# A two-round graph network on one core: the rows that TensorE gathers are made four halves ahead instead of eight

## The chip, the cores and the metric

The kernel runs on one core of one Trainium2 chip. The metric is the device time of one execution, in microseconds (us). The kernel before takes 5044.6 us, the median of three runs (5039.53, 5044.60 and 5044.64).

## What is computed

There are 12500 nodes of 16 numbers and 400000 edges, each with a source node, a target node and 13 edge features. The targets are sorted. The reference, cut to what matters:

```
w = relu(edge_attr @ w1 + b1) @ w2 + b2        # per edge a 16 x 16 matrix W, once
for _ in range(2):                             # two rounds
    m   = einsum('ei,eio->eo', hx[edge_src], W)
    agg = segment_sum(m, edge_dst) / max(degree, 1)
    hx  = gru_cell(agg, hx)                    # two 16 x 48 matrices, sigmoid, tanh
out = layernorm(x + hx)
```

The change is in `hx[edge_src]`, the gather of the source rows.

## The kernel before

**Tiles.** The edges are cut into tiles of 128. 64 tiles are a super (NSUP = 49 supers), and a super is worked off in 8 halves of 8 tiles, k = 0 to 7. Each of the two rounds runs over the 49 supers. The loops are unrolled for the first pair of supers and for the last super (`for_supers`, L420), so `is_first` means super 0 of a round and `is_last` means super 48. In time, the supers are counted through here: 0 to 48 are those of round 0 and 49 to 97 those of round 1.

**A half, engine by engine.** The gathered rows of a half lie in xg. VectorE multiplies them with a one-hot of the target's place in a window into `fan` (`spread`, L1184). TensorE multiplies `fan` with the hidden layer of the edges (`products`, L805). In round 0 TensorE also makes the hidden layer of the next super (`hidden`, L780), which is stored to h_d by SP (L513) and loaded again in round 1 (L529). At places of a super set by k, TensorE also runs `own_sums` (k = 0 and 6), `aggregate` (k = 0), `turn` (k = 2) and `scatter` (k = 4 and 5).

**Two ways to gather.** Of the 8 tiles of a half, POOL gathers 5 (or 4) by one indirect DMA each (L598), and TensorE makes the other 3 (or 4; `BY_PE`, L33: 24 tiles a super in round 0, 26 in round 1). For these, ScalarE makes a one-hot of the sources from the broadcast keys (`src_hots`, L655: four Abs and one Relu). TensorE multiplies it with the node table in SBUF, seven matmuls a tile (`gather_rows`, L783). VectorE picks the row out of 28 candidates (`pick_rows`, L1222, one instruction a tile) with a mask made once a super (`rows_hot`, L1210), and sums (`keep_rows`, L1230, one a half). TensorE's tiles are made one super ahead: during half k of super s, those of half k of super s + 1. So super 0 of a round has none made by TensorE: POOL gathers all its 64 tiles (`pool_places`, L106), and the last super has no gather work on TensorE. There it runs the 12 node-side gate products instead, 2 a half from k = 2 (`side_gates`, L856), and ScalarE copies them out (`keep_sides`, L673).

**What sets the order.** Each engine has its own list of instructions and waits on semaphores. POOL may run LEAD = 4 halves ahead of `products` (L595). VectorE's order in a half is: spread, one-hot of the next half, keep_hot, (add_windows at k = 5 and 6), pick and keep of the gather of the half before, `rows_hot` at k = 0, and `places` at k = 2. In supers 0 and 1 of round 0 it also runs `relative` (L1125 to L1130) in each half.

**SP's queue.** SP issues, for super `sup`: the indices (L473), the features (L485), the keys of super sup + 1 (L506), then in round 0 the store of the hidden layer, in round 1 its load. Ahead of the keys it waits that the buffer is free:

```
wait_pos(sp, s_src_hot, pe_total(rnd) if is_first(i, par) else pe_count(rnd, sup, 0))   # L503
```

In super 1 of round 0 there follow, behind the keys, `loads_of_later()` (L446: 15 small `lane` copies, `meta`, 8 `slot_of` broadcasts, weights), the first store to h_d, and two DMAs that zero the accumulator acc_all (L519). VectorE waits for these at the end of super 0: `places_of_tiles()`, then `dve.wait_ge(s_acc, 32)` (L1302). After this comes the drain that tells all engines that the super is done.

Of the kernel before, what the change touches and what calls it, by code (L numbers as in the profile page):

```python
# [5 lines left out]
P = 128  # L6
# [27 lines left out]
LEAD = 4  # L34
DUO = 2
# [11 lines left out]
KB = 4  # L47
# [14 lines left out]
def gnn_program(nc, x, x_t, src_tiles, src_pe_rows, src_pe_cols, dst_rows, dst_tiles, ef_t, w1_diag, w2_io, w2_oi,  # L62
# [30 lines left out]
    assert 6 * GW <= PICKED and GN <= SLOTS * C * AR and 4 * GN <= TG * P * 4 // 2 * 2  # L93
    assert NSUP % 2 == 1 and NSUP <= P and GROUPS * C == P and 2 * GN == NT and C == 16
# [24 lines left out]
    def keys_use(rnd, i, par):  # L119
        buf, use = ring(rnd, i, par)  # L120
        return use - sum(ring(r, 0, 0)[0] == buf for r in range(rnd + 1))
# [20 lines left out]
    with ExitStack() as ctx:  # L142
# [229 lines left out]
        SIDE_FROM, SIDE_EACH = 2, 2  # L372
# [62 lines left out]
        def is_last(i):  # L435
            return isinstance(i, int) and i == PAIRS

# [7 lines left out]
        def _(sp):  # L445
# [21 lines left out]
            for rnd in range(ROUNDS):  # L467
                def emit(i, par, rnd=rnd):
# [150 lines left out]
        def _(act):  # L619
# [35 lines left out]
            def src_hots(rnd, i, par, s, k):  # L655


                buf, use = ring(rnd, i, par)
                first, some = sum(GT[:k + 1]) - BY_PE[rnd][k], BY_PE[rnd][k]
                if k == 0:  # L660
                    act.wait_ge(s_keys[buf], 16 * keys_use(rnd, i, par))
                if k > 1:
                    act.wait_ge(s_g, pe_count(rnd, s, sum(BY_PE[rnd][:k - 1])))
                else:
                    wait_pos(act, s_g, pe_count(rnd, s, 0) - (1 - k) * (0 if isinstance(s, int) and s == 1 else BY_PE[rnd][HPS - 1]))
# [3 lines left out]
                act.wait_ge(s_src_far, KB * (HPS * (rnd * (NSUP - 1) + s - 1) + k + 1))  # L669
# [43 lines left out]
            for rnd in range(ROUNDS):  # L713

                def emit(i, par, rnd=rnd):
                    sup = rnd * NSUP + 2 * i + par
                    buf, _ = ring(rnd, i, par)
                    for k in range(HPS):
                        if k == 0 and not is_last(i):
                            src_hots(rnd, i + par, 1 - par, 2 * i + par + 1, 0)  # L720
                        if k == 0 and not is_first(i, par):
                            keep_agg(sup - 1)
                        if k > 0 and k + 1 < HPS and not is_last(i):
                            src_hots(rnd, i + par, 1 - par, 2 * i + par + 1, k + 1)
# [9 lines left out]
                        if not is_last(i) and k == 0:  # L734
# [799 lines left out]
```

## Time and profile before

| what | us |
|---|---|
| median of the runs (3) | 5044.6 |
| span of the profiled execution, first to last instruction | 5034.4 |
| median less span (start and end of the program) | 10.2 |
| round 0 to the first fan of its last super | 0 to 2493.8 |
| last super of round 0, its tail and the node update | 2493.8 to 2584.2 |
| first super of round 1 (super 49) | 2584.2 to 2662.2 |
| rest of round 1 to the first fan of the last super | 2662.2 to 4942.8 |
| last super of round 1 and the end | 4942.8 to 5034.4 |

The time of the profiled execution itself is not given apart from its span; the sum is made against the span, and what lies around the span is taken as unchanged. In the tables of busy time a window runs from the first fan of a super to the next stage's first fan. In the timeline a line gives the start, the time taken, the engine and line of code, what is written and read, how many instructions are merged, and in brackets how long the engine sat idle before it and what ended that.

### The profile page before, as it was taken

The numbers are of one execution on the slowest core, as the hardware profiler recorded it, in microseconds if no ns is written. First come the engines' busy times: TensorE is split into PE (matmuls) and PEld (weight loads), VectorE is DVE, ScalarE is ACT, GpSimd is POOL, SyncE is SP. The second block draws the span as 40 slices with busy tenths as digits, with TensorE's granted clock in tenths as the row PEclk, the third lists the DMA queues.
The fourth block names the chain that finished last, engine by engine and source line by source line (L and its number), as shares of the span: only waits on it lengthen the run. The fifth ranks groups of instructions, "written<-read, shape, count | busy, mean of one in ns | idle before, by whom it ended". The sixth has DMA issues, their size and how long they took to land.

```text
span 5034.4 us, 125092 instructions
## 1 busy us (share of the span) xinstructions
PE 4872.1 (97%) x41816; PEld 4032.3 (80%) x41817; DVE 4440.1 (88%) x6732; ACT 3310.7 (66%) x5283; POOL 3666.9 (73%) x3879
## 2 busy tenths in 40 slices
PE   6999999999999999999969999999999999999997
PEld 4788888878888878888748888888888888888885
DVE  8888888888888888888848999999999999999996
ACT  4667676766666666666636767667677676766763
POOL 7677777777777777777757777777777777777773
PEclk9999999999999999999979999999999999999998
DMA  6122222212122212121111111111111111111110
GB/s 164 46 58 53 56 55 55 56 51 61 50 62 50 61 46 65 46 65 46 51 50 55 39 55 39 55 55 39 55 39 55 55 40 55 39 55 46 48 48 17
DMA packets 193534, 269.20 MB, mean 53 GB/s; under 512 B 93601, under 2 KB 161796, under 8 KB 180065
## 3 DMA queue, kind: packets, MB, share of 16 engines
q1 hardware_dynamic: 62353, 223.38, 13.4%
q0 software_dynamic: 123584, 31.88, 6.1%
q8 instruction: 373, 6.11, 0.5%
q10 hardware_dynamic: 7026, 6.21, 0.5%
q14 instruction: 198, 1.62, 0.1%
HBM read 201.25 MB, written 54.94 MB: 51 GB/s over the span
## 4 chain that ended last, share of the span: by engine, by line
PE 91%; issue 3%; DVE 3%; POOL 2%; DMA 1%; DVEq 0%; POOLq 0%; ACT 0%; ACTq 0%; SPq 0%
PE ps_all L793 58%; PE ps_all L805 10%; PE ps_all L795 9%; PE ps_all L780 5%; PE ps_all L828 4%; PE ps_all L849 2%; POOL xg L598 2%; PE ps_all L819 1%; PE ps_all L835 1%; DVE shared L1222 1%; DVE fan L1184 1%; DVE xg L1230 0%; DMA acc_all<-in_dst_rows 0%; DMA stat_all<-low_d 0%; PE ps_all L854 0%
## 5 line engine op out<-in xcount | busy, mean ns | idle before, releaser
L793 PE MATMUL ps_all<-parts,src_hot 128*128 128x448 f32 x14400 | 3417.8, 373 | 8.2 <-DVEq L1108 7.0
L793 PEld LDWEIGHTS ps_all<-parts,src_hot 128*128 128x128 f32 x14400 | 2665.4, 188 | 324.5 <-issue 103.3
L598 POOL DMA_INDIRECT xg<-in_x,idx x1979 | 1874.6, 947 | 641.5 <-issue 554.6
L598 POOL DMA_INDIRECT xg<-h_rows,idx x1883 | 1777.3, 944 | 627.2 <-issue 532.1
L667 ACT ACTIVATE src_hot<-keys,neg_key 128x384 fp32r<-128x384 int16 (+1 forms) x3072 | 1680.3, 620 | 794.9 <-PE ps_all L795 785.8
L1222 DVE TENSOR_TENSOR shared<-ps_all,at_hot 128x448 f32<-128x448 f32 x2400 | 1390.2, 616 | 287.3 <-PE ps_all L795 264.9
L1230 DVE TENSOR_REDUCE xg<-shared 128x48 f32<-128x1344 f32 (+1 forms) x768 | 1237.5, 1611 | 81.8 <-DVE shared L1222 3.3
L1184 DVE TENSOR_TENSOR fan<-xg,ps_all 128x1280 f32<-128x1280 f32 x784 | 1159.5, 1479 | 119.7 <-DMA xg<-h_rows,idx 49.1
L671 ACT ACTIVATE src_hot<-src_hot 128x1536 fp32r<-128x1536 f32 (+1 forms) x768 | 1184.9, 1543 | 74.4 <-ACT src_hot L667 8.2
L795 PE MATMUL ps_all<-parts,src_hot 128*128 128x448 f32 x2400 | 878.8, 366 | 0.0
L805 PE MATMUL ps_all<-fan,h_sb 128*32 128x160 f32 x12544 | 592.6, 307 | 82.9 <-DVE fan L1184 80.5
L805 PEld LDWEIGHTS ps_all<-fan,h_sb 128*32 128x32 f32 x12544 | 328.7, 109 | 338.6 <-issue 274.0
L795 PEld LDWEIGHTS ps_all<-parts,src_hot 128*128 128x128 f32 x2400 | 451.5, 188 | 37.6
L639 ACT COPY shared<-ps_all 128x320 f32<-128x320 f32 x784 | 326.9, 417 | 234.7 <-PE ps_all L805 234.6
L645 ACT COPY agg_sb<-ps_all 128x160 f32<-128x160 f32 x98 | 28.7, 293 | 484.3 <-PE ps_all L828 484.3
L780 PE MATMUL ps_all<-w_sb,ef 105*128 105x264 f32 x784 | 285.7, 447 | 29.0 <-DMA ef<-in_ef_t 20.8
L828 PE MATMUL ps_all<-shared,w2s 128*64 128x160 f32 x3136 | 240.3, 307 | 1.9 <-issue 1.9
L780 PEld LDWEIGHTS ps_all<-w_sb,ef 105*128 105x128 f32 x784 | 119.0, 191 | 131.2 <-issue 117.8
L828 PEld LDWEIGHTS ps_all<-shared,w2s 128*64 128x64 f32 x3136 | 209.9, 139 | 7.4 <-issue 2.2
L1172 DVE TENSOR_TENSOR ps_all<-ps_all,rel 128x80 f32<-128x80 f32 x784 | 189.8, 242 | 0.2 <-DVE ps_all L1161 0.2
L1191 DVE COPY hot_sb<-ps_all 128x80 f32<-128x80 f32 x784 | 180.2, 230 | 0.0
L633 ACT ACTIVATE h_sb<-ps_all 128x264 f32<-128x264 f32 x392 | 154.2, 393 | 30.0 <-PE ps_all L780 24.3
(135 smaller groups left out, 1284.8 us busy)
## 6 DMA issues: line engine op xcount, KB each, us to landing
keys<-key_d SPq DMA_DIRECT2D x96, 832.0 KB
h_d<-h_sb SPq DMA_DIRECT2D x49, 1056.0 KB
h_sb<-h_d SPq DMA_DIRECT2D x49, 1056.0 KB
xg<-in_x,idx POOLq DMA_INDIRECT x1979, 2.3
xg<-h_rows,idx POOLq DMA_INDIRECT x1883, 2.3
ef<-in_ef_t SPq DMA_DIRECT2D x49, 420.0 KB
acc_all<-agg_t SPq DMA_DIRECT2D x1, 3161.0 KB
idx<-in_src_tiles SPq DMA_DIRECT2D x98, 32.0 KB, 1.8
```

Of the source, the lines that this page charges most:

```text
L598: pool.indirect_dma_start(out=xg[:, buf, at, 0:C], out_offset=None, in_=rows_of, in_offset=bass.IndirectOffsetOnAxis(ap=idx[:, buf, at:at ...
L639: act.copy(pev[:, :, 2 * k:2 * k + 2, :].rearrange("p i u n -> p u i n"), ps_p[k % 2][:, 0:2 * C * WIN].rearrange("p (u i n) -> p u i n", ...
L667: act.activation(src_hot[k % 2][:, kb, 0:some * P], keys[:, buf, first * P:(first + some) * P], ACT.Abs, bias=neg_key[:, kb:kb + 1]).then_ ...
L671: act.activation(hot_of, hot_of.bitcast(F32), ACT.Relu, bias=1.0, scale=-1.0).then_inc(s_src_hot, some)
L780: pe.matmul(ps_h[:, 0:HT * HA], ef[:, buf, k, :], w1_sb[:], start=True, stop=True).then_inc(s_h, 1)
L793: pe.matmul(ps_g[j], src_hot[k % 2][:, kb, j * P:(j + 1) * P], parts[:, m * WHOLE + kb, :], start=(kb == 0 and m == 0), stop=False)
L795: last = pe.matmul(ps_g[j], src_hot[k % 2][:, WHOLE, j * P:(j + 1) * P], tail_part, start=False, stop=True)
L805: last = pe.matmul(ps_p[k % 2][b * HID:(b + 1) * HID, u * C * WIN:(u + 1) * C * WIN], h_sb[:, buf, k * HT + u * BPS + b, 0:HID], fan[:, k ...
L828: last = pe.matmul(ps_agg[lo:lo + BPS * C, 0:TPB * WIN], w2s[:, i, :], pev[:, i].rearrange("p t n -> p (t n)"), start=(i < 2), stop=(i >= ...
L1184: dve.tensor_tensor(fan[:, k % 2], xg[:, buf, k * HT:(k + 1) * HT, 0:C].unsqueeze(3).to_broadcast([P, HT, C, WIN]), hot[:, k % 2].unsqueez ...
L1222: dve.tensor_tensor(picked[:, j], ps_g[j].rearrange("p (a c) -> p c a", a=AR), at_hot[:, u].unsqueeze(1).to_broadcast([P, C, AR]), ALU.mul ...
L1230: dve.tensor_reduce(xg[:, buf, at:at + many, 0:C], picked[:, 0:many], AX_X, ALU.add).then_inc(s_xg_pe, many)
```

## The change

The gather on TensorE runs EARLY = 4 halves ahead: during half k, the rows of half k + 4 are made, of the same super for k < 4 and of the next one for k >= 4. Halves 4 to 7 of super 0 of each round then have 3 or 4 tiles made by TensorE, and so do not need POOL for them. The gather of the last super's halves 4 to 7 is made in its halves 0 to 3. The side gates move from 2 a half from k = 2 to 4 a half from k = 5. `rows_hot` for super 0 runs at k = 0 of super 0, that for super s + 1 at k = 4 of super s. SP loads the keys of super 0 too, and its wait ahead of the keys counts the tiles anew: `pe_count(rnd, sup, 0)` is 12 larger than before in round 0 (12 tiles of super 0 are counted now, of its 24), so for super 1 it asks for 12 where it asked for 0.

```diff
+EARLY = 4
+SIDE_FROM, SIDE_EACH = 5, 4
     def pool_places(rnd, s, k):
-        made = 0 if isinstance(s, int) and s == 0 else BY_PE[rnd][k]
+        made = 0 if isinstance(s, int) and s == 0 and k < EARLY else BY_PE[rnd][k]
...
+    def skipped(rnd):
+        return sum(BY_PE[rnd][:EARLY])
 
     def pe_total(rnd):
-        return (NSUP - 1) * sum(sum(BY_PE[r]) for r in range(rnd))
+        return sum(NSUP * sum(BY_PE[r]) - skipped(r) for r in range(rnd))
 
     def pe_count(rnd, s, n):
-        return pe_total(rnd) + (s - 1) * sum(BY_PE[rnd]) + n
+        return pe_total(rnd) + s * sum(BY_PE[rnd]) + n - skipped(rnd)
...
-        SIDE_FROM, SIDE_EACH = 2, 2
...
+        def rows_for(i, par, k):
+
+            if k + EARLY < HPS:
+                return i, par, k + EARLY
+            return None if is_last(i) else (i + par, 1 - par, k + EARLY - HPS)
+
+        def rows_before(i, par, k):
+
+            if k > 0:
+                return rows_for(i, par, k - 1)
+            return None if is_first(i, par) else (i, par, EARLY - 1)
+
+        def rows_next(i, par, k):
+
+            if k + 1 < HPS:
+                return rows_for(i, par, k + 1)
+            return None if is_last(i) else (i + par, 1 - par, EARLY)
...
                     if not is_last(i):
                         wait_pos(sp, s_src_hot, pe_total(rnd) if is_first(i, par) else pe_count(rnd, sup, 0))
-                        if is_first(i, par) and rnd > 0:
-                            sp.wait_ge(s_rz_sum, NS * rnd)
+                        if is_first(i, par):
+                            if rnd > 0:
+                                sp.wait_ge(s_rz_sum, NS * rnd)
+                            sp.dma_start(keys[:, buf, :], key_d[0:1, :].to_broadcast([P, TG * P])).then_inc(
+                                s_keys[buf], 16)
...
-                        if k == 0 and not is_last(i):
-                            src_hots(rnd, i + par, 1 - par, 2 * i + par + 1, 0)
+                        if k == 0 and is_first(i, par):
+                            src_hots(rnd, *rows_for(i, par, 0))
...
-                        if k > 0 and k + 1 < HPS and not is_last(i):
-                            src_hots(rnd, i + par, 1 - par, 2 * i + par + 1, k + 1)
+                        if k > 0 and rows_next(i, par, k):
+                            src_hots(rnd, *rows_next(i, par, k))
...
-                        if not is_last(i) and k == 0:
-                            src_hots(rnd, i + par, 1 - par, 2 * i + par + 1, 1)
+                        if k == 0:
+                            src_hots(rnd, *rows_next(i, par, k))
...
-                        if not is_last(i):
+                        if rows_for(i, par, k):
                             if is_first(i, par) and k == 0:
                                 pe.wait_ge(s_parts, rnd + 1)
-                            gather_rows(rnd, s + 1, k)
+                            gather_rows(rnd, *rows_for(i, par, k))
...
+                        made = rows_before(i, par, k)
+                        if made:
+                            pick_rows(rnd, *made, (0, 1))
...
+                        if made:
+                            pick_rows(rnd, *made, (2, 3))
+                            keep_rows(rnd, *made)
...
-                        if not is_last(i) and k == 0:
+                        if is_first(i, par) and k == 0:
+                            rows_hot(rnd, 0)
+                        if not is_last(i) and k == EARLY:
                             rows_hot(rnd, s + 1)
```

Left out of the diff are the waits of `src_hots`, `gather_rows`, `pick_rows` and `rows_hot`, which take the new counts.

## Rows read from the trace of the kernel before

**Rows 1.** The page: busy time of each engine, and the chain that ended last.

```profile
PE 4872.1 (97%) x41816; PEld 4032.3 (80%) x41817; DVE 4440.1 (88%) x6732; ACT 3310.7 (66%) x5283; POOL 3666.9 (73%) x3879
PE 91%; issue 3%; DVE 3%; POOL 2%; DMA 1%; DVEq 0%; POOLq 0%; ACT 0%; ACTq 0%; SPq 0%
```

**Rows 2.** Busy time by stage: PE, PEld, DVE, ACT, POOL, granted clock, DMA share, GB/s.

```profile
2443.40:2493.80 50.40, 50.40 (x429) 40.98 (x429) 43.89 (x66) 33.25 (x57) 37.78 (x41) 1.00 0.20 48
2493.80:2524.00 30.20, 23.92 (x283) 14.75 (x281) 21.03 (x37) 9.15 (x21) 18.83 (x20) 0.94 0.14 40
2584.20:2662.20 78.00, 50.90 (x327) 41.50 (x328) 45.84 (x78) 33.49 (x48) 58.89 (x63) 0.81 0.11 23
4894.50:4942.80 48.30, 48.30 (x428) 41.40 (x426) 45.38 (x68) 31.51 (x46) 35.86 (x38) 1.00 0.13 31
4942.80:4971.00 28.20, 22.63 (x284) 14.29 (x282) 21.54 (x38) 9.06 (x21) 16.99 (x18) 1.00 0.19 36
```

**Rows 3.** Waits of the whole run (page, costliest groups): what fan waits for.

```profile
L1184 DVE TENSOR_TENSOR fan<-xg,ps_all 128x1280 f32<-128x1280 f32 x784 | 1159.5, 1479 | 119.7 <-DMA xg<-h_rows,idx 49.1 <-DVE xg L1230 44.5 <-issue 17.7
```

**Rows 4.** Timeline at the start of round 1: POOL's issues, and fans of super 49.

```profile
2574.43 0.94 POOL L598 DMA_INDIRECT xg<-h_rows,idx  x1 [0.30 <-issue]
...
2614.46 1.49 DVE L1184 TENSOR_TENSOR fan<-xg,ps_all 128x1280 f32<-128x1280 f32 x1 [4.02 <-DMA xg<-h_rows,idx]
...
2654.49 1.49 DVE L1184 TENSOR_TENSOR fan<-xg,ps_all 128x1280 f32<-128x1280 f32 x1 [5.01 <-DMA xg<-h_rows,idx]
```

**Rows 5.** SP's issues in super 0 of round 0.

```profile
39.38 0.62 SPq L506 DMA_DIRECT2D keys<-key_d  x1
...
59.21 18.20 SPq L519 DMA_DIRECT2D acc_all<-agg_t  x2
```

**Rows 6.** Busy time in two short windows of super 0; last but one is the DMA share.

```profile
95.00:100.00 5.00, 5.00 (x55) 4.22 (x53) 4.76 (x8) 2.10 (x4) 3.78 (x5) 1.00 0.43 92
100.00:105.00 5.00, 4.54 (x34) 3.62 (x34) 4.83 (x11) 3.42 (x7) 3.78 (x5) 1.00 0.07 10
```

**Rows 7.** Timeline of super 0: ScalarE's fourth one-hot, and VectorE's end of the super.

```profile
70.51 1.49 ACT L671 ACTIVATE src_hot<-src_hot 128x1536 fp32r<-128x1536 f32 x1
...
106.50 0.42 DVE L1152 TENSOR_SCALAR slot_of<-slot_of,lane 128x392 f32<-128x392 f32 x1
```

**Rows 8.** Timeline of a steady super of round 1: halves 5 to 7, then rows_hot at k = 0.

```profile
3673.04 1.69 DVE L1222 TENSOR_TENSOR shared<-ps_all,at_hot 128x448 f32<-128x448 f32 x3
...
3674.41 1.47 PE L793 MATMUL ps_all<-parts,src_hot 128*128 128x448 f32 x6
...
3678.50 1.68 DVE L1222 TENSOR_TENSOR shared<-ps_all,at_hot 128x448 f32<-128x448 f32 x3
...
3679.52 1.48 PE L793 MATMUL ps_all<-parts,src_hot 128*128 128x448 f32 x6
...
3688.35 0.91 DVE L1210 TENSOR_TENSOR at_hot<-ps_all,at_pe 128x728 f32<-128x728 f32 x1
...
3689.18 1.48 DVE L1184 TENSOR_TENSOR fan<-xg,ps_all 128x1280 f32<-128x1280 f32 x1
```

**Rows 9.** Waits of L1222, ten steady supers of round 0, then twelve of round 1.

```profile
DVE shared L1222 <- PE ps_all L795: 47.4, 79, 1.8
...
DVE shared L1222 <- PE ps_all L795: 12.8, 36, 0.5
```

**Rows 10.** Timeline of the last super of round 0: two gathers, first and last products, gates.

```profile
2493.64 1.38 PE L793 MATMUL ps_all<-parts,src_hot 128*128 128x448 f32 x6
...
2495.07 1.38 PE L793 MATMUL ps_all<-parts,src_hot 128*128 128x448 f32 x6
...
2496.58 0.75 PE L805 MATMUL ps_all<-fan,h_sb 128*32 128x160 f32 x16
...
2521.86 0.75 PE L805 MATMUL ps_all<-fan,h_sb 128*32 128x160 f32 x16 [2.48 <-DVE fan L1184]
...
2522.54 1.58 PE L854 MATMUL ps_all<-mh,gate_w 128*128 128x392 f32 x4
```

More of the change, by code:

```diff
@@ L93, in gnn_program @@
     assert 6 * GW <= PICKED and GN <= SLOTS * C * AR and 4 * GN <= TG * P * 4 // 2 * 2
+    assert EARLY % 2 == 0 and 0 < EARLY < HPS and SIDE_FROM > HPS - EARLY
     assert NSUP % 2 == 1 and NSUP <= P and GROUPS * C == P and 2 * GN == NT and C == 16
@@ L117, in landed, with starts_round @@
         return i * (16 * usual) + 16 * (earlier + usual + first + last)
-    def keys_use(rnd, i, par):
-        buf, use = ring(rnd, i, par)
-        return use - sum(ring(r, 0, 0)[0] == buf for r in range(rnd + 1))
+    def skipped(rnd):
+        return sum(BY_PE[rnd][:EARLY])
     def pe_total(rnd):
-        return (NSUP - 1) * sum(sum(BY_PE[r]) for r in range(rnd))
+        return sum(NSUP * sum(BY_PE[r]) - skipped(r) for r in range(rnd))
     def pe_count(rnd, s, n):
-        return pe_total(rnd) + (s - 1) * sum(BY_PE[rnd]) + n
+        return pe_total(rnd) + s * sum(BY_PE[rnd]) + n - skipped(rnd)
+    def starts_round(s, k):
+        return isinstance(s, int) and s == 0 and k == EARLY
     def slot_free(rnd, k, j):
@@ L653, in keep_turned, with src_hots @@
                              s_agg_t, 1)
[L655 removed]
+            def src_hots(rnd, i, par, k):
                 buf, use = ring(rnd, i, par)
+                s = 2 * i + par
                 first, some = sum(GT[:k + 1]) - BY_PE[rnd][k], BY_PE[rnd][k]
[L660 to L662 removed]
+                if k == 0 or starts_round(s, k):
+                    act.wait_ge(s_keys[buf], 16 * use)
+                if isinstance(s, int) and s == 0 and k < EARLY + 2:
+                    wait_pos(act, s_g, pe_total(rnd))
+                elif k > 1:
                     act.wait_ge(s_g, pe_count(rnd, s, sum(BY_PE[rnd][:k - 1])))
                 else:
[L665 removed]
+                    act.wait_ge(s_g, pe_count(rnd, s, 0) - (1 - k) * BY_PE[rnd][HPS - 1])
                 for kb in range(KB):
@@ L781, in hidden, with gather_rows @@
                           start=True, stop=True).then_inc(s_h, 1)
-            def gather_rows(rnd, s, k):
+            def gather_rows(rnd, i, par, k):
+                s = 2 * i + par
                 for j, (n, _, _) in enumerate(pe_tiles(rnd, k)):
                     pe.wait_ge(s_src_hot, pe_count(rnd, s, n) + 1)
-                    if isinstance(s, int) and s == 1 and slot_free(rnd, k, j) < 0:
+                    if isinstance(s, int) and s == 0 and slot_free(rnd, k, j) < skipped(rnd):
                         wait_pos(pe, s_picked, pe_total(rnd))
@@ L1181, in spread @@
                 dve.wait_ge(s_xg[buf][k], landed(rnd, i, par, k))
-                if not is_first(i, par):
+                if not (is_first(i, par) and k < EARLY):
                     dve.wait_ge(s_xg_pe, pe_count(rnd, 2 * i + par, sum(BY_PE[rnd][:k + 1])))
@@ L1207, in rows_hot @@
             def rows_hot(rnd, s):
-                wait_pos(dve, s_picked, pe_count(rnd, s, 0))
+                wait_pos(dve, s_picked, pe_total(rnd) if isinstance(s, int) and s == 0 else pe_count(rnd, s, 0))
                 dve.tensor_tensor(at_hot[:], iota_ps[:, 0:AR].unsqueeze(1).to_broadcast([P, TG, AR]),
@@ L1212, in rows_hot, with pick_rows @@
                                   ALU.is_equal).then_inc(s_at_hot, 1)
-            def pick_rows(rnd, s, k, js):
+            def pick_rows(rnd, i, par, k, js):
+                s = 2 * i + par
                 for j, (n, u, _) in enumerate(pe_tiles(rnd, k)):
                     if j in js:
-                        if n == 0:
-                            dve.wait_ge(s_at_hot, rnd * (NSUP - 1) + s)
+                        if n == 0 or j == 0 and starts_round(s, k):
+                            dve.wait_ge(s_at_hot, rnd * NSUP + s + 1)
                         dve.wait_ge(s_g, pe_count(rnd, s, n) + 1)
```

17 lines of the change are left out of this document (3 added, 14 removed).

## The prediction

> **What bounds the kernel now.** I read the page first: TensorE is busy 97% of the span and 91% of the chain that ended last [rows 1]. A mean over stages does not say what one edit is worth, so I then cut the span by supers, from the first fan of one to the first fan of the next [rows 2]. There are three regimes. In a steady super TensorE is busy all the time: 50.4 of 50.4 us in round 0, 48.3 of 48.3 in round 1. In the last super of a round it has no gather and is busy 23.9 of 30.2 us (22.6 of 28.2 in round 1). In the first super of round 1 it is busy 50.9 of 78.0 us. Third, the waits: fan waits 49.1 us in all for gathered rows to land [rows 3], and the timeline puts nearly all of it into super 49 [rows 4]: there POOL gathers 8 tiles a half at 0.94 + 0.30 = 1.25 us, 10.0 us a half, and from half 3 to half 7 the fans stand 40.0 us apart over four halves. POOL is close behind TensorE elsewhere (40 issues x 1.25 = 49.9 us of a 50.4 us super), but fan does not wait for it there. Fourth, SP's queue at the start [rows 5] and VectorE's margins in a steady super [rows 8, 9], since the change moves things past both.
>
> **The start of round 1.** Halves 4 to 7 of super 49 lose 3 + 3 + 3 + 4 = 13 indirect DMAs. 13 x 1.25 = 16.2 us. The cover is thin but there: with 5 issues a half lasts 6.2 us on POOL, and VectorE needs some 5 us (fan 1.5 [rows 3], one-hot and copy 0.3, three picks 1.7 [rows 8], sum 1.5) and 0.8 more once for rows_hot, TensorE 3 x 1.43 [rows 10] + 0.75 = 5.0. The first super of round 1 does as many gathers on TensorE as before (26). SP now loads the keys of two supers, 832 KB more, just before h_rows is complete; beside the stores of h_rows that may hold POOL's start by up to 2 us, and I take 1. Sum: -15 us, between -17 and -8.
>
> **The start of round 0.** Here POOL was not the limit: it starts at once and has 46 us before the first fan. So its 12 fewer issues give nothing; VectorE bounds supers 0 and 1. But SP is moved past a new wait. For super 1 the wait ahead of the keys asks for 12 one-hots, where it asked for none. Those are halves 4 to 7 of super 0, and ScalarE ends the fourth at 70.51 + 1.49 = 72.0 us [rows 7]. Before, SP went through at 39.38 [rows 5]. Everything behind it is 32.6 us late: lane, meta, slot_of, the weights, the store to h_d, and the two DMAs that zero acc_all, which were issued at 59.2 and go out at about 91.8. How long do these take? The DMA engines are loaded until the window 95 to 100, where the share has fallen to 0.43, and at 100 to 105 it is 0.07, the level of the gathers alone [rows 6]: the fill ended at about 98.5, 39.3 us after its issue. So it would end at 131. VectorE is through with slot_of at 106.9 [rows 7] and then waits for the fill; one more rows_hot (0.9, [rows 8]) makes that 107.8. The wait is 131 - 107.8 = 23 us where it was none, and with the rows_hot the term is +24. Who waits: all, since the drain behind it releases POOL, SP and TensorE for super 1. Nothing gives it back, since supers 0 and 1 are VectorE's and the rest TensorE's. Bounds: the 15 lane copies could issue faster on a quiet queue and save some us, the clock falls while TensorE idles and could cost some: +15 to +30.
> The fill is 4791 KB in rows of 872 bytes. The Trainium skill (DMA: Bandwidth & Descriptors, Anatomy of one DMA) fits a DMA (of GpSimd's queue) as 2.0 us plus its bytes at 436 GB/s; that would be 13 us, an estimate, and the fill would end at 105, before VectorE asks for it, and this term would be +1. The trace does not agree: the share stays up for three times as long.
>
> **A steady super.** The gather counts are the same in every half (the round-1 pattern 3, 3, 3, 4 repeats after four halves), and the order on TensorE and ScalarE too. Two things move. SP's keys now go at half 2 of the super before instead of at its start, and the store to h_d (round 0) or the load of h_sb (round 1) behind them also. Both are needed a super's start later; some 30 us are left, and the DMA share is back at the gathers' level some 8 us after such issues: nothing. The other is rows_hot, from k = 0, where TensorE has own_sums and aggregate beside it, to k = 4. It takes VectorE 3689.18 - 3688.35 = 0.83 us [rows 8] and pushes the picks of halves 5, 6 and 7. TensorE may not overwrite a bank before it is picked. In round 0 VectorE has time: its picks wait for TensorE 47.4 us in ten supers, 4.7 each [rows 9]. In round 1 it is 12.8 in twelve, 1.1 each, and none of it in halves 5 to 7. There the first pick of half 7 ends at 3678.50 + 0.62 = 3679.12, and the gather that reuses its bank starts at 3679.52: 0.40 us of margin; in half 6 3674.41 - 3673.66 = 0.75. Pushed by 0.83, half 6 is short by 0.1 and half 7 by 0.4 in all; with 0.1 for the release I take 0.5 us a super. At k = 0 VectorE catches up again (margin there is over 2 us, and rows_hot is gone), so it is paid once in each of supers 50 to 96: 47 x 0.5 = +23 us. Bounds: nothing, if VectorE regains the 0.83 before half 7, and 47 x 0.9 = +42, if nothing of it is covered.
>
> **The last supers.** 12 and 13 gather tiles come in. Their pitch is 2495.07 - 2493.64 = 1.43 us [rows 10]: 17.2 and 18.6 us of TensorE. TensorE's idle time in these windows was 30.2 - 23.9 = 6.3 and 28.2 - 22.6 = 5.6 us, and no more than that can be hidden: +10.9 to +17.2, and +13.0 to +18.6. Step by step for round 0: from the first products to the gates' end it was 2496.58 to 2524.1, 27.5 us [rows 10]. Now the first four halves go at steady pace less the hidden layers, 24.4 us, and halves 4 to 7 have products (0.75), two scatters (0.7), own_sums (0.5) and 12 gates at about 0.75 (two in 1.58), with fan ready in time: about 16 us. 40.4 - 27.5 = +13. Round 1 the same with one more tile and no hidden layer before: +15. The gates are only moved, and fit between, as TensorE is the bound there anyway; POOL's 4 issues a half (5.0 us) now hide below it.
>
> **The sum.** -15 + 24 + 23 + 13 + 15 = +60. On the span that is 5034.4 + 60 = 5094.4, and with the 10.2 us around it, 5104.6. The span plus 10.2 is the median of the runs by construction, and the other runs lie at most 5 us below it. 0.2%, about 10 us, is what a measurement of this kernel can tell from no change.
>
> **Rivals.** First, the fill of acc_all lands in time, or nearly (the DMA share of 95 to 105 is then not its end but the gathers', and it was done at 85 or so): the term is +1 instead of +24, and the time 5082. For it: the rule above; against: the share. Second, VectorE absorbs the moved rows_hot in round 1: the term is 0, the time 5081. For it: it waits 1.1 us a super somewhere; against: none of that lies in the three halves that follow. Both together: 5058. Third, on the other side: POOL is the true pacer. Its 40 x 1.25 us of each 50.4 leave half a microsecond, and if fan waits hidden in TensorE's busy time are really POOL's, then each issue less is worth its 1.25 us in both rounds, 25 x 1.25 = 31 us, and the gathers of the last super fit under POOL's pace there. It decides from the point where POOL, not the picks, releases fan in the steady supers; with no new stall at the start that is 5013. Against it: fan's 49.1 us of such waits are nearly all in super 49. Fourth, worse: the late rows_hot costs its full 0.9 in round 1 and the restart after a 23 us idle stretch runs at 1.2 GHz for some halves (in super 49 the mean granted clock was 0.81 [rows 2]): +20 and +5, 5130. That the change does not do what it says is not open: the counts follow from the code.
>
> **Chances.** The forecast with all five terms 0.56; fill in time 0.12; rows_hot absorbed 0.16; both 0.05; worse 0.05; POOL the pacer 0.02; the rest, 0.04, near no change: the last supers cost little and one of the two stalls is missing. Faster by over 0.2% 0.03, within it 0.03, slower 0.94. The range takes in the first three cases with their bounds: 5072 to 5122.
>
> **What would show it.** Right: in the profile after, VectorE idles some 23 us before the first fan of super 1, released by the DMA of acc_all, and SP's keys for super 2 go out at about 72. The fans of halves 4 to 7 of super 49 stand 6.2 us apart. The supers of round 1 last 48.8 instead of 48.3 and TensorE's gather waits for the pick L1222 by some 0.4 us each, those of round 0 stay at 50.3. The last supers last some 40 from first products to last gate. Wrong: no idle time before super 1, or a super of round 1 at 48.3, or last supers below 35.

## The result and the profile after

The kernel after takes 5108.77 us, the median of four runs (5103.34 to 5110.54), against 5044.62 (5039.53 to 5047.11) beside it: a ratio of 1.0126, 95% interval 1.0114 to 1.0138. That is slower, by 64 us. The profiled execution took 5103.34 us and its span is 5101.4, so only 1.9 us lie around the span, and the span has grown by 67.0. The three us between 64 and 67 come from which execution was profiled: spans alone are compared below, and they hold some us that belong to the single execution.

The page of after: busy time by engine, the chain that ended last, and the costliest groups that changed.

```profile
PE 4912.7 (96%) x41991; PEld 4054.3 (79%) x41992; DVE 4471.2 (88%) x6767; ACT 3330.4 (65%) x5323; POOL 3652.3 (72%) x3854
...
PE 76%; DVE 10%; issue 8%; DVEq 3%; DMA 2%; POOL 1%; SPq 0%; ACT 0%; POOLq 0%; ACTq 0%
...
L822 PE MATMUL ps_all<-parts,src_hot 128*128 128x448 f32 x14550 | 3452.2, 373 | 29.2 <-DVE shared L1252 21.7
...
L1213 DVE TENSOR_TENSOR fan<-xg,ps_all 128x1280 f32<-128x1280 f32 x784 | 1159.6, 1479 | 108.8 <-DVE xg L1261 41.0
```

Against [rows 1], TensorE's share of the chain fell from 91% to 76% and VectorE's rose from 3% to 10%. TensorE's gather now waits 21.7 us for the picks of L1252, and fan's largest releaser is no longer the DMA of gathered rows, as it was in [rows 3], but VectorE's own sum.

I cut both spans at the same places, by the times at which the fans start, and subtracted:

| stretch | before | after | difference | predicted |
|---|---|---|---|---|
| start to the first fan | 46.9 | 44.8 | -2.1 | 0 |
| super 0 | 61.5 | 83.9 | +22.4 | +24 |
| super 1 | 60.1 | 61.0 | +0.9 | 0 |
| supers 2 to 47 | 2325.4 | 2323.4 | -1.9 | 0 |
| last super of round 0 to the first fan of round 1 | 90.4 | 105.2 | +14.8 | +13 |
| super 49 | 77.9 | 63.8 | -14.1 | -15 |
| supers 50 to 96 | 2280.7 | 2315.2 | +34.6 | +23 |
| last super of round 1 and the end | 91.6 | 104.1 | +12.5 | +15 |
| sum | | | +67.1 | +60 |

How far one trace can differ from another where nothing was changed is seen in b_sp_wait and b_gates_late_2 (below), whose steady supers are those of before: supers 50 to 96 take 2286.2 and 2286.0 us there, 5 us more than here. So +34.6 is rather +29 by those two, and a last super is known to within some 2 us.

**Start of round 0.** SP's issues in after, to be read against [rows 5].

```profile
68.78 0.33 SPq L531 DMA_DIRECT2D keys<-key_d  x1
70.18 11.17 SPq L476 DMA_DIRECT2D lane<-lane  x15
...
86.63 17.04 SPq L544 DMA_DIRECT2D acc_all<-agg_t  x2
```

VectorE after it has finished slot_of:

```profile
104.57 0.42 DVE L1181 TENSOR_SCALAR slot_of<-slot_of,lane 128x392 f32<-128x392 f32 x1
128.68 1.49 DVE L1213 TENSOR_TENSOR fan<-xg,ps_all 128x1280 f32<-128x1280 f32 x1 [23.68 <-issue]
```

Busy time in three short windows of super 0 (PE, PEld, DVE, ACT, POOL, granted clock, DMA share, GB/s):

```profile
95.00:100.00 5.00, 4.95 (x37) 3.75 (x35) 4.81 (x12) 3.12 (x6) 3.78 (x5) 1.00 0.93 147
...
120.00:125.00 5.00, 0.00 (x0) 0.00 (x0) 0.00 (x0) 0.00 (x0) 3.65 (x4) 0.50 0.79 138
125.00:130.00 5.00, 0.00 (x0) 0.00 (x0) 1.32 (x1) 0.00 (x0) 0.00 (x0) 0.50 0.13 23
```

The keys went out at 68.78 instead of 39.38, the fill of acc_all at 86.63 instead of 59.21. The DMA share is at 0.79 in 120 to 125 and 0.13 in 125 to 130, with only the fill's tail and four gathers in the first of the two windows: the fill ended some 39 us after its issue, as in [rows 6]. VectorE sat idle for 23.68 us, and TensorE's granted clock was at 0.50 meanwhile. The wait shows as "issue", not as a DMA: the row alone does not name the fill, its place behind slot_of and the window do.

**A steady super of round 1**, from rows_hot, which now runs at k = 4, to half 7; its counterpart is [rows 8].

```profile
3699.83 0.91 DVE L1239 TENSOR_TENSOR at_hot<-ps_all,at_pe 128x728 f32<-128x728 f32 x1
3700.65 1.48 DVE L1213 TENSOR_TENSOR fan<-xg,ps_all 128x1280 f32<-128x1280 f32 x1
...
3709.59 1.46 PE L822 MATMUL ps_all<-parts,src_hot 128*128 128x448 f32 x6 [0.21 <-DVE shared L1252]
...
3715.05 1.45 PE L822 MATMUL ps_all<-parts,src_hot 128*128 128x448 f32 x6 [0.27 <-DVE shared L1252]
```

TensorE stalls 0.21 us in half 6 and 0.27 in half 7 for a bank that is not picked yet. In this super halves 0 to 3 last 25.13 us against 25.14 in one of before, halves 4 to 7 last 23.82 against 23.29: +0.53. The waits of after in twelve such supers (total, times, longest):

```profile
DVE shared L1252 <- PE ps_all L824: 21.7, 40, 3.1
PE ps_all L822 <- DVE shared L1252: 5.1, 24, 0.3
```

TensorE waits 5.1 / 12 = 0.43 us a super, two places each, where before no such wait was listed in this stretch. The supers grew by 0.57 us in the median (48.44 to 49.01) and by 0.74 in the mean (34.6 / 47). By halves, from fan to fan in the median, half 4 grew from 6.39 to 7.32 (the mask's new place), half 0 fell from 6.77 to 5.95 (its old one), and half 1 grew from 6.41 to 6.95; the others kept their length. So VectorE is late through halves 5 to 7, makes it good in half 0, and what TensorE lost meanwhile comes out in half 1. One more super than before lasts some 52 us: super 69, at 51.9 against 49.3. Ahead of its first fan VectorE idles 3.5 us in after and 3.9 in before, so the pause is not new; in after TensorE also stops for 2.19 us within the products that follow. The cause of either is open.

**The stages around the turn of the round and at the end**, from first fan to first fan or to the last fan and its gates, against [rows 2].

```profile
2462.60:2513.10 50.50, 50.50 (x431) 41.06 (x430) 43.83 (x67) 34.26 (x59) 37.90 (x41) 1.00 0.17 46
2513.10:2549.40 36.30, 33.47 (x290) 26.18 (x292) 32.63 (x50) 16.50 (x29) 18.89 (x20) 0.95 0.13 36
2618.30:2682.10 63.80, 46.50 (x327) 38.56 (x328) 46.52 (x78) 32.60 (x47) 48.51 (x51) 0.81 0.15 38
...
4997.40:5036.00 38.60, 35.33 (x345) 28.51 (x344) 35.15 (x54) 16.74 (x29) 16.40 (x18) 1.00 0.13 26
```

A steady super of round 0 stays as it was (50.5 us). Super 49 is 14 us shorter. In both last supers TensorE is no longer idle for a fifth of the time, and VectorE is busy for most of it too: 32.6 of 36.3 us and 35.2 of 38.6 busy, against 21.0 of 30.2 before. Where the 14.8 us of the last super of round 0 went: from its first fan to its last it takes 34.3 us against 26.5, and from the last fan to the end of the last scatter 15.3 against 9.8. The ten us behind the last fan, before and then after:

```profile
2520.32:2530.32 10.00, 6.82 (x104) 4.92 (x104) 4.10 (x8) 3.33 (x7) 0.00 (x0) 1.00 0.01 2
```

```profile
2547.37:2557.37 10.00, 10.00 (x125) 5.72 (x125) 3.57 (x5) 6.70 (x14) 0.00 (x0) 1.00 0.01 2
```

There TensorE works without a pause and VectorE is mostly idle. The fans of super 49's halves 3, 4, 5 and 6 and what they waited for:

```profile
2651.93 1.49 DVE L1213 TENSOR_TENSOR fan<-xg,ps_all 128x1280 f32<-128x1280 f32 x1 [8.26 <-DMA xg<-h_rows,idx]
...
2656.89 1.48 DVE L1213 TENSOR_TENSOR fan<-xg,ps_all 128x1280 f32<-128x1280 f32 x1
...
2666.39 1.48 DVE L1213 TENSOR_TENSOR fan<-xg,ps_all 128x1280 f32<-128x1280 f32 x1
...
2671.33 1.48 DVE L1213 TENSOR_TENSOR fan<-xg,ps_all 128x1280 f32<-128x1280 f32 x1
```

Half 3 is late, after a wait of 8.26 us. POOL's issues and SP's, in super 49 (the first of POOL's and the 32nd, which is the last of half 3, then SP's load of keys and hidden layer for super 50):

```profile
2607.08 0.95 POOL L623 DMA_INDIRECT xg<-h_rows,idx  x1 [12.49 <-DMA h_rows<-xg]
...
2646.18 0.95 POOL L623 DMA_INDIRECT xg<-h_rows,idx  x1 [0.30 <-issue]
```

```profile
2644.45 0.33 SPq L531 DMA_DIRECT2D keys<-key_d  x1
2644.88 0.38 SPq L554 DMA_DIRECT2D h_sb<-h_d  x1
```

POOL holds its pitch of 1.25 us up to there. The page gives 2.3 us from such an issue to landing, so the fan could have run at some 2649; it ran at 2651.93. SP's two loads went out 2 us before the last gather of half 3, and the DMA share is at 0.65 around it (first window below). From half 3 to half 7 (2676.28) it takes 24.4 us, where [rows 4] had 40.0, but not evenly: 5.0, 9.5, 4.9, 4.9. Against before, half 3 is 3.4 us late, the four halves behind it save 15.7, and the last one 1.8: together -14.1. The 9.5 has a reason of its own, in the same columns as the windows above:

```profile
2644.00:2653.00 9.00, 1.66 (x9) 1.17 (x7) 1.06 (x1) 4.35 (x7) 6.86 (x8) 0.80 0.65 222
2653.00:2660.00 7.00, 6.52 (x31) 5.35 (x32) 6.09 (x11) 0.44 (x1) 5.17 (x7) 0.53 0.06 6
2660.00:2682.00 22.00, 21.84 (x187) 18.52 (x186) 19.71 (x28) 15.79 (x23) 16.82 (x18) 1.00 0.07 8
```

TensorE idles 7.8 us behind the late half 3, then the granted clock is 0.53 for 7 us (31 matmuls where full speed makes some 60), then 1.00.

### The profile page after: what moved, and what is told of

Same layout as the page of the kernel before. It is cut to its first block, busy times and chain, and to the rows that moved or that the text cites. A ratio compares the mean times of both kernels' runs of the same rounds, so it can differ in the third digit from the quotient of the medians.

```text
span 5101.4 us, 125792 instructions
## 1 busy us (share of the span) xinstructions
PE 4912.7 (96%) x41991; PEld 4054.3 (79%) x41992; DVE 4471.2 (88%) x6767; ACT 3330.4 (65%) x5323; POOL 3652.3 (72%) x3854
## 4 chain that ended last, share of the span: by engine, by line
PE 76%; DVE 10%; issue 8%; DVEq 3%; DMA 2%; POOL 1%; SPq 0%; ACT 0%; POOLq 0%; ACTq 0%
PE ps_all L822 48%; PE ps_all L824 8%; PE ps_all L834 8%; PE ps_all L808 5%; PE ps_all L857 4%; DVE shared L1252 4%; DVE fan L1213 3%; DVEq L1276 2%; PE ps_all L878 1%; PE ps_all L848 1%; PE ps_all L864 1%; DMA acc_all<-agg_t 1%; POOL xg L623 1%; DVE ps_all L1201 1%; DVE acc_all L1281 1%
## 5 line engine op out<-in xcount | busy, mean ns | idle before, releaser
L822 PE MATMUL ps_all<-parts,src_hot 128*128 128x448 f32 x14550 | 3452.2, 373 | 29.2 <-DVE shared L1252 21.7
L695 ACT ACTIVATE src_hot<-keys,neg_key 128x384 fp32r<-128x384 int16 (+1 forms) x3104 | 1698.5, 619 | 930.3 <-PE ps_all L824 924.3
L1252 DVE TENSOR_TENSOR shared<-ps_all,at_hot 128x448 f32<-128x448 f32 x2425 | 1403.5, 618 | 323.0 <-PE ps_all L824 307.3
L1261 DVE TENSOR_REDUCE xg<-shared 128x48 f32<-128x1344 f32 (+1 forms) x776 | 1250.5, 1612 | 85.9 <-DVE shared L1252 7.6
L699 ACT ACTIVATE src_hot<-src_hot 128x1536 fp32r<-128x1536 f32 (+1 forms) x776 | 1197.0, 1543 | 73.3 <-ACT src_hot L695 4.3
L824 PE MATMUL ps_all<-parts,src_hot 128*128 128x448 f32 x2425 | 888.6, 366 | 0.0
```

The source lines that it names most:

```text
L695: act.activation(src_hot[k % 2][:, kb, 0:some * P], keys[:, buf, first * P:(first + some) * P], ACT.Abs, bias=neg_key[:, kb:kb + 1]).then_ ...
L699: act.activation(hot_of, hot_of.bitcast(F32), ACT.Relu, bias=1.0, scale=-1.0).then_inc(s_src_hot, some)
L822: pe.matmul(ps_g[j], src_hot[k % 2][:, kb, j * P:(j + 1) * P], parts[:, m * WHOLE + kb, :], start=(kb == 0 and m == 0), stop=False)
L824: last = pe.matmul(ps_g[j], src_hot[k % 2][:, WHOLE, j * P:(j + 1) * P], tail_part, start=False, stop=True)
L1252: dve.tensor_tensor(picked[:, j], ps_g[j].rearrange("p (a c) -> p c a", a=AR), at_hot[:, u].unsqueeze(1).to_broadcast([P, C, AR]), ALU.mul ...
L1261: dve.tensor_reduce(xg[:, buf, at:at + many, 0:C], picked[:, 0:many], AX_X, ALU.add).then_inc(s_xg_pe, many)
```

## The experiments

The theory is the prediction's: separate terms that add up. Its rivals are named in the expectations. Each kernel is measured beside before on the same chip. Where a kernel is compared with after, the first figure is the difference of the medians, and the one behind it takes each against the before beside it. The first four ran beside a before of 5041.73 us (5035.93 to 5044.84, 7 runs).

**The wait of SP alone, in the kernel before** (b_sp_wait).

```diff
@@ before, behind L503
+                        if rnd == 0 and isinstance(i, int) and i == 0 and par == 1:
+                            sp.wait_ge(s_src_hot, 12)
```

> The kernel before with one wait added: SP waits for 12 one-hots ahead of the keys of super 2, at the start of round 0. My theory (the fill of acc_all behind this wait is what VectorE waits for at the end of super 0): +20 to +23 us over the kernel before, about 5066; the first fan of super 1 moves from 108 to about 129, and SP passes the keys at about 72. Rival (the lost time at the start belongs to the gather four halves ahead, not to SP's queue): within 3 us of the kernel before, 5045.

Measured: 5063.61 (5060.06 to 5069.53), ratio 1.0043 (1.0027 to 1.0060), +21.9 us. SP's issues and the first fan of super 1:

```profile
70.90 0.33 SPq L508 DMA_DIRECT2D keys<-key_d  x1
...
89.12 18.58 SPq L521 DMA_DIRECT2D acc_all<-agg_t  x2
```

```profile
130.00 1.49 DVE L1186 TENSOR_TENSOR fan<-xg,ps_all 128x1280 f32<-128x1280 f32 x1 [23.76 <-issue]
```

The wait alone, with nothing else of the change, makes the whole stall of 23.8 us. Super 0 lasts 83.1 us, as in after.

**After, with the loads ahead of SP's wait** (a_loads_first): in super 1 of round 0 the wait and the keys behind it move behind the fill.

```diff
@@ after, L524 and behind L546
-                    if not is_last(i):
+                    late_keys = rnd == 0 and isinstance(i, int) and i == 0 and par == 1
+                    if not is_last(i) and not late_keys:
...
+                    if late_keys:
+                        wait_pos(sp, s_src_hot, pe_total(rnd) if is_first(i, par) else pe_count(rnd, sup, 0))
+                        sp.dma_start(keys[:, 1 - buf, :],
...
```

> The changed kernel with SP's wait and the keys of super 2 moved behind the fill of acc_all. My theory: the 21 us stall at the end of super 0 is gone, 5108.8 - 21 = 5088; SP issues the fill at about 59 as in the kernel before. Rival (the fill is slow for another reason, or the halves 4 to 7 of super 0 cost VectorE the time): 5105 or more.

Measured: 5086.98 (5085.41 to 5090.52), ratio 1.0094 (1.0078 to 1.0111), 21.8 us below after (18.9). The fill goes out early again, and the stall before the first fan of super 1 is gone, but for 1.4 us:

```profile
59.61 18.24 SPq L545 DMA_DIRECT2D acc_all<-agg_t  x2
77.89 14.67 SPq L550 DMA_DIRECT2D keys<-key_d  x1
```

```profile
108.97 1.49 DVE L1219 TENSOR_TENSOR fan<-xg,ps_all 128x1280 f32<-128x1280 f32 x1 [1.42 <-issue]
```

Adding the wait costs 21.9 us and removing it gives 19 to 22 back, so this term is shown from both sides. Super 0 lasts 61.7 us, as long as in before (61.5).

**An extra rows_hot at k = 4, in the kernel before** (b_mask_extra). Nobody reads it; the true one stays at k = 0. at_hot becomes two buffers in bf16, so that both fit.

```diff
@@ before, L209 and L1290
-        at_hot = sb("at_hot", [P, TG, AR])
+        at_hot = sb("at_hot", [P, 2, TG, AR], mybir.dt.bfloat16)
...
+                        if not is_last(i) and k == 4:
+                            wait_pos(dve, s_at_more, rnd * (NSUP - 1) + s)
+                            dve.tensor_tensor(at_hot[:, 1], iota_ps[:, 0:AR].unsqueeze(1).to_broadcast([P, TG, AR]),
...
```

> The kernel before with a second mask operation of the same size at k = 4 of every super, whose result nobody reads (the mask is kept in bf16 to make room, so the picks read bf16). My theory (0.83 us of VectorE between half 4 and half 5 runs into the bank reuse of halves 6 and 7 in round 1): supers of round 1 go from 48.5 to about 49.1 to 49.3 us, those of round 0 stay at 50.3, +27 to +35 us in all, about 5075. Rival (the longer supers of round 1 come from the shorter lead, from SP's later transfers or from ScalarE): 5045, supers at 48.5.

Measured: 5070.88 (5067.77 to 5075.80), ratio 1.0061 (1.0044 to 1.0078), +29.2 us. The supers of round 1 last 49.1 us, those of round 0 50.5 as before. The wait that after has is there in the same twelve supers, and it was not in before:

```profile
PE ps_all L794 <- DVE shared L1223: 6.1, 25, 0.6
```

**After, with the mask back at k = 0** (a_mask_two): two buffers, and rows_hot for super s + 1 runs at k = 0 of super s, as in before, while the gather keeps its lead of four.

```diff
@@ after, L214, L1253 and L1315
-        at_hot = sb("at_hot", [P, TG, AR])
+        at_hot = sb("at_hot", [P, 2, TG, AR], mybir.dt.bfloat16)
...
-                                          at_hot[:, u].unsqueeze(1).to_broadcast([P, C, AR]),
+                                          at_hot[:, par, u].unsqueeze(1).to_broadcast([P, C, AR]),
...
-                        if not is_last(i) and k == EARLY:
-                            rows_hot(rnd, s + 1)
+                        if not is_last(i) and k == 0:
+                            rows_hot(rnd, s + 1, 1 - par)
```

> The changed kernel with two mask buffers (bf16), so that rows_hot stays at k = 0. My theory: supers of round 1 return to 48.5 us, -27 to -35 us, about 5078. Rival (the shorter lead or SP's later transfers cost the 0.6 to 0.7 us a super): 5105 or more, supers at 49.1.

Measured: 5082.54 (5076.94 to 5085.65), ratio 1.0081 (1.0064 to 1.0098), 26.2 us below after (23.3). Supers of round 1 are back at 48.4 us, and TensorE's wait for the pick is gone from the list of the twelve supers. Supers 50 to 96 take 2288.9 us in all, 26.3 less than in after, and in b_mask_extra 2312.9, 26.7 more than in b_sp_wait beside it. So the place of one instruction of 0.9 us on VectorE is worth 26 to 27 us over round 1 by these traces, 23 to 29 by the medians, and nothing in the other round. The picks take the same time from a bf16 mask (618 ns each, against 616 and 618 from fp32), so the type of the mask is not what was measured.

**Four runs that give no sizes.** a_both, b_fewer_pool, a_one_matmul and b_gates_late went to one chip on which the kernel before itself took 6591.03 us (6577.38 to 6614.12, 19 runs), at a clock of about 0.90 and with waits for a remote party on ScalarE, VectorE and GpSimd, as this one for ACT in the listing of a_both:

```profile
L701 ACT ACTIVATE src_hot<-keys,neg_key 128x384 fp32r<-128x384 int16 (+1 forms) x3104 | 1696.9, 620 | 1751.7 <-remote 963.1
```

Their expectations and ratios stand here; three were repeated on another chip, and what follows rests on those.

> The changed kernel with both repairs (the fill ahead of the keys wait, two mask buffers). My theory: what is left of the change is -14 in the first super of round 1 and +13 to +15 in each last super, so 5044.6 + 13 = about 5055 (5050 to 5060). Rival (the last supers cost less once VectorE has time): 5045 or less.

Ratio 0.9904 (0.9875 to 0.9933).

> The kernel before with the 13 indirect DMAs of halves 4 to 7 of super 0 in round 1 left out (those rows keep what round 0 left in them; nothing makes them). This is the gain of the change alone, without its price. My theory (POOL's pace bounds that super): its halves 4 to 7 go from 10.0 to about 6.2 us, -14 to -17 us, about 5029. Rival (VectorE or TensorE is close behind POOL there): -5 or less.

Ratio 0.9979 (0.9966 to 0.9992). The sign fits the prediction's step; the size stays unmeasured by an experiment of its own, and rests on super 49 of after.

> The changed kernel with the gather of the last super of each round cut to one matmul a tile instead of seven (12 and 13 tiles; their rows are left wrong). My theory (the last supers are longer by the gather's matmuls on TensorE): -10 us a round, 5108.8 - 20 = about 5088, first four halves of the last super at 3 to 5 us each. Rival (VectorE's picks and sums, 3.2 us a half, or the late side gates bound them): -8 or less in all.

Ratio 0.9893 (0.9874 to 0.9913).

> The kernel before with the side gates at 4 a half from k = 5 instead of 2 from k = 2. My theory: they cost little by their place, +1 to +4 us a round, 5047 to 5053. Rival (the late gates carry most of the last super's longer time): +8 or more a round.

Ratio 1.0018 (1.0005 to 1.0031).

The four kernels below ran beside a before of 5042.01 us (5037.98 to 5051.99, 19 runs).

**Both repairs** (a_both_2): the two edits of a_loads_first and a_mask_two together.

> The same kernel as in a_both, on a chip where the kernel before takes its usual time. The two repairs gave 21.8 and 26.2 us alone, and they act in different places, so together 5109 - 48 = 5061 (5056 to 5066) if my theory holds that what is left is the last supers less the first super of round 1. Rival (they overlap, since VectorE's time is one resource): 5070 or more.

Measured: 5056.59 (5053.53 to 5061.60), ratio 1.0026 (1.0016 to 1.0036), +14.6 us. The repairs took 21.8 and 26.2 us off the 64 singly (18.9 and 23.3), which leaves 16 (22): they add up, as closely as these runs can tell. The stretches of its profile: last super of round 0 and tail 107.1 us, super 49 62.9, supers of round 1 48.71 in the mean (before 48.53), last super of round 1 and end 106.0. Against before that is +16.7, -15.0, +8.5 and +14.5, some 25 us, because the profiled execution is the slowest of its nine; the median is 14.6 above. What is left is the trade that the lead of four makes: super 49 gains once what the last super loses twice.

**The last supers' gathers cut to one matmul a tile** (a_one_matmul_2).

```diff
@@ after, L820 and L825
-                    for kb in range(WHOLE):
+                    short = is_last(i)
+                    for kb in range(0 if short else WHOLE):
...
-                                     start=False, stop=True)
+                                     start=short, stop=True)
```

> The same kernel as in a_one_matmul: the gather of the last super of each round cut to one matmul a tile (its rows are wrong). Theory (the matmuls themselves lengthen the last supers): about 10 us a round less, 5088. Rival (the picks and sums on VectorE and the late gates carry most of it): 5098 or more.

Measured: 5100.25 (5097.16 to 5102.62), ratio 1.0111 (1.0094 to 1.0128), 8.5 us below after (5.9), with intervals that overlap; the rival forecast this. 25 tiles x 6 matmuls are left out, some 25 x 1.24 = 31 us of TensorE's time at full clock, and little comes back: the last super and tail of round 0 last 106.7 us against 105.2 in after and 106.1 to 107.1 in its repaired variants, and those of round 1 104.3 against 104.1. TensorE now waits for fan in each half, as in this one:

```profile
2533.25 1.29 PE L835 MATMUL ps_all<-fan,h_sb 128*32 128x160 f32 x16 [2.64 <-DVE fan L1214]
```

and VectorE in the same halves, from fan to fan:

```profile
2536.66 1.48 DVE L1214 TENSOR_TENSOR fan<-xg,ps_all 128x1280 f32<-128x1280 f32 x1
2538.05 0.24 DVE L1202 TENSOR_TENSOR ps_all<-ps_all,rel 128x80 f32<-128x80 f32 x1
2538.20 0.23 DVE L1221 COPY hot_sb<-ps_all 128x80 f32<-128x80 f32 x1
2538.35 1.68 DVE L1253 TENSOR_TENSOR shared<-ps_all,at_hot 128x448 f32<-128x448 f32 x3
2540.13 1.55 DVE L1262 TENSOR_REDUCE xg<-shared 128x48 f32<-128x1344 f32 x1
2541.60 1.48 DVE L1214 TENSOR_TENSOR fan<-xg,ps_all 128x1280 f32<-128x1280 f32 x1
```

There is no gap in it: 4.94 us a half, of which picks and sum are the 3.2 that the change has moved here. That is so in halves 3 and 4; halves 1 and 2 take 5.5 and 6.2 here and 7.8 and 6.4 in after. And TensorE, with less to do, got half the clock:

```profile
2525.70:2549.60 23.90, 16.20 (x100) 8.61 (x100) 21.82 (x34) 9.77 (x18) 10.53 (x12) 0.50 0.05 4
```

so that the products (16 in 1.29 us instead of 0.75) and the gates are slower too. From the first fan to the last this stage is 2.5 us shorter than in after (31.8 against 34.3), and from the last fan to its end 4.0 longer (74.9 against 70.9). So the run did two things at once: it took matmuls away, and the clock fell. What the matmuls would be worth at full clock it does not show. The first gates, here and in after:

```profile
2545.46 4.91 PE L884 MATMUL ps_all<-mh,gate_w 128*128 128x392 f32 x8
```

```profile
2546.03 3.33 PE L883 MATMUL ps_all<-mh,gate_w 128*128 128x392 f32 x8
```

**The gates late, in the kernel before** (b_gates_late_2).

```diff
@@ before, L372
-        SIDE_FROM, SIDE_EACH = 2, 2
+        SIDE_FROM, SIDE_EACH = 5, 4
```

> The kernel before with the side gates 4 a half from k = 5. The changed kernel's timeline shows the last products waiting some 4 us behind gates. Theory A (the gates' place costs little without the gathers): +1 to +3 us a round. Theory B (twelve gates in three halves are on the chain, whatever else): +5 to +7 us a round, 5052 to 5058.

Measured: 5046.08 (5043.21 to 5049.76), ratio 1.0007 (0.9998 to 1.0017): +4.1 us, some 2 a round, and the interval holds no change. By itself the move of the gates is at most a small part of the 12 to 15 us that a last super has grown by. Theory B falls. What the late gates cost beside the gathers was not tested.

**A lead of six with both repairs** (a_six_both): two halves of the last super and of super 49 would move instead of four.

```diff
@@ a_both_2, L35
-EARLY = 4
-SIDE_FROM, SIDE_EACH = 5, 4
+EARLY = 6
+SIDE_FROM, SIDE_EACH = 4, 3
```

> Both repairs and a lead of six halves instead of four, side gates 3 a half from k = 4. Theory (gain and price go with the halves moved): half the gain in super 49 (-8), and the gather in the last super only in halves 0 and 1, where TensorE had 6 us idle, so +2 to +5 a round: about 5044 to 5048, no difference to the kernel before. Rival (the price goes with the gates being late and not with the halves): 5055.

Measured: 5062.47 (5057.88 to 5064.51), ratio 1.0034 (1.0020 to 1.0049), +20.5 us, a miss. The last supers did halve their cost (98.9 and 99.3 us, against 107.1 and 106.0 with a lead of four) and super 49 kept 9.6 of its 15.0 us of gain (68.3), more than the half that was expected. But the supers of round 1 lasted 49.04 us in the mean against 48.71, which over 47 of them is 16 us (in the median 48.72 against 48.43). BY_PE of round 1 has a period of four halves. A lead of four leaves the 4-tile halves where they were, a lead of six moves them to k = 1 and k = 5, beside `places` on VectorE at k = 2, and TensorE waits for a pick there:

```profile
3662.55 1.47 PE L828 MATMUL ps_all<-parts,src_hot 128*128 128x448 f32 x6 [0.17 <-DVE shared L1258]
```

In twelve such supers these waits are 2.0 us in all, 0.17 a super, and a_both_2 has none; half 2, where `places` runs, takes 8.39 us in the median against 6.40. That the shifted pattern is the cause is argued from this and was not tested by turning the pattern with the lead. On the chips that ran before at its usual time, no kernel here beat it. Making halves 4 to 7 of super 49 on top of an unchanged lead of eight was not tried.

## Why the prediction was right, and where its steps were not

- **Sign and sum.** +60 was predicted; it measured +64 on the medians and +67 on the spans. 5108.77 lies in the range, 4 us above the forecast. All five terms have the predicted sign. On the spans the errors are -5 us at the start of round 0 with the stretches around it, +1 at the start of round 1, +12 in the steady supers, +2 and -3 in the last ones: one term carries the miss, and some 5 of its 12 us are the difference between single executions.
- **Start of round 0, +24: right in mechanism and close in size.** Two experiments show it. It came 2 us shorter in that stretch: the fill was issued at 86.6, not 91.8, because ScalarE ended the fourth one-hot at 67.26 + 1.49 = 68.75, not at 72.0, and SP's keys followed at 68.78, and the 15 lane copies took 11.2 us, not 12.8. VectorE was through with slot_of at 104.99, not 107.8, so its wait kept the forecast size (23.68 against 23). With the stretches around it the net is +19 to +21.
- **The rule against it.** The rival that the fill lands in time gave 5082; it fell. The fill took some 39 us a second time. The Trainium skill's fit for a DMA of GpSimd's queue (DMA: Bandwidth & Descriptors, Anatomy of one DMA) would give 13 us, an estimate; the trace does not agree, here as in before.
- **Start of round 1, -15: right in size, in part for another reason.** The step put halves 4 to 7 6.2 us apart, at POOL's pace. They are 5.0, 9.5, 4.9 and 4.9. The 1 us that it took off for a later start of POOL did not come: POOL's first gather starts 11.1 us ahead of the first fan in before and 11.2 in after. POOL had the five gathers of half 4 issued by 2652.44 + 0.94, and from there no fan waits for it; VectorE set the pace, and the one long half is TensorE at 0.53 of its clock after 7.8 us of idleness. Two misses, which together came out at about 6.1 a half, by luck. The step that called the moved keys and the load behind them free failed here: they now go out at half 2 of super 49, beside gathers that the fan is waiting for, and half 3 came some 3 us late. Other traces bear this out: in a_six_both the two loads go out 8.0 and 11.4 us into super 49, and half 3 is at POOL's pace again (30.35 us into the super, in before 30.21, in after 33.66), while half 1 comes at 12.38, against 11.48 in a_both_2. No run moved the loads alone.
- **Steady supers of round 1, +23: right mechanism, term too small.** It measured +34.6. The stall itself is as predicted, at the picks of halves 6 and 7, 0.43 us a super against 0.5. The term took nothing else to be slower; the super grew by 0.57 in the median and 0.74 in the mean. The traces of b_mask_extra and a_mask_two put 26 to 27 us on the place of rows_hot. The other 8 are in a_both_2 too, which has the mask back at k = 0: its mean super is 0.18 us above before, its median (48.43) is not. Some 5 us of the 8 are also in b_sp_wait and b_gates_late_2, whose steady supers are those of before. That leaves some 3 us, as much as super 69 is longer in a_both_2 than in before (52.0 against 49.3); its cause is open. The forecast of 23 was thus short by some 3 us of what the mask costs. The rival that VectorE absorbs the move fell.
- **Last supers, +13 and +15: sizes right (+14.8, +12.5), reason incomplete.** The step gave TensorE as the bound. The step-by-step sum holds: from the first products to the gates' end it is 2515.82 to 2556.7, 40.9 us, where 40.4 was forecast. But a_one_matmul_2 shows that taking TensorE's work away gives little back: the picks and the sum, which came along with the gathers and which the prediction did not price on VectorE in these supers, make a chain of 4.9 us a half, as long as TensorE's work in halves 3 and 4. That the two were equal there is luck, and part of why the number fitted; the other part is the stretch behind the last fan, where TensorE is the bound as forecast (10.0 of 10.0 us busy). How much is due to each is open, since the clock fell in that run. "The gates fit between" is not so in after: alone, their move cost some 2 us a round at most, but beside the gathers eight of the twelve run behind the last fan, four of them in front of the last products:

```profile
2550.27 2.90 PE L883 MATMUL ps_all<-mh,gate_w 128*128 128x392 f32 x8
2553.11 0.75 PE L834 MATMUL ps_all<-fan,h_sb 128*32 128x160 f32 x16
```

Fan 7 was ready at 2547.37 + 1.49 = 2548.86; its products start 4.2 us later, behind half 6's products, own_sums and these gates.
- **POOL as the pacer: fell.** In a_loads_first POOL has twelve gathers fewer in super 0 of round 0, and super 0 lasts 61.7 us against 61.5; and the gathers of the last supers did not fit under POOL's pace. In the steady supers POOL issues as much as before, so they say nothing on this.
- **The 10.2 us around the span** were not that. After shows 1.9 us. In the other runs of before the span is some 2.1 us below the time, so the execution that was profiled took about 5036.5, an estimate, 8 us under the median. For the forecast of the time this cancels, since it is the median plus the sum.

## What to carry to other kernels

When a producer's lead is renumbered, go through every wait that counts its output and list what is queued behind it on its engine: here one wait on a loading queue cost 19 to 22 us through a fill that has nothing to do with the gather. An instruction moved on an engine that is 94% busy must be priced against the shortest buffer margin behind its new place, not against the engine's mean idle time. Work taken out of an idle stretch at one end of a pipeline comes back at the other, once a round, together with what its consumers do on other engines; count both engines before calling one the bound. When a lead is changed, see where it moves the heavy steps of the work pattern; that keeping it at a multiple of the pattern's period helps was not tested here.

## What the runs showed of the hardware

Where TensorE was relieved of matmuls (a_one_matmul_2), its clock was lower and the stage no shorter: with 16.2 of 23.9 us busy the granted clock was 0.50 (1.2 GHz), and 16 products took 1.29 us instead of 0.75; in after it was 0.95 with 33.5 of 36.3 us busy. After it had idled 7.8 us in super 49, the clock was 0.53 over the next 7 us. The fill of acc_all, 4791 KB, took about 39 us from issue to end whether it started at 59, at 87 or (b_sp_wait) at 89 us. And one chip ran the same kernel before in 6591 us, 31% longer, with waits for a remote party on ScalarE, VectorE and GpSimd, and the ratio of the same two kernels came out up to 2.2 per cent apart (a_one_matmul 0.9893, a_one_matmul_2 1.0111). What disturbed it is not known.
